# A causal bound at 64 tokens in a fused attention stage: 1280 instead of 1536 score columns a head step, new masks, sums and value layout

## The chip, the cores and the metric

The kernel runs as one program on one core of a Trainium2 chip. A core has five engines that run their own instruction streams in order and wait for each other on semaphores: TensorE (PE, matrix products into PSUM), VectorE (DVE), ScalarE (ACT), GpSimd (POOL) and SyncE (SP, which issues the transfers). The metric is device time in microseconds (us) of one execution; lower is better.

## The reference, cut to what matters

The network normalises and convolves a sequence, applies a mixture of experts, then attention, then the mixture of experts again, each with a residual sum. The change lies in the attention:

```python
def _L0_attn_b_ref(x, W_attn, W_proj):      # x: 16 batches, 256 tokens, 128 channels
    N_HEAD, N_QUERY_SETS = 16, 4            # 4 query sets share one set of keys and values, hd = 8
    qkv = x @ W_attn.T
    parts = jnp.split(qkv, N_QUERY_SETS + 2, axis=-1)
    causal = jnp.tril(jnp.ones((Tz, Tz), dtype=bool))
    for g in range(N_QUERY_SETS):
        att = jnp.einsum('bhqd,bhkd->bhqk', q, k) * scale
        att = jnp.where(causal, att, -jnp.inf)
        att = jax.nn.softmax(att, axis=-1)
        y = jnp.einsum('bhqk,bhkd->bhqd', att, v)
        outs.append(y.transpose(0, 2, 1, 3).reshape(Bz, Tz, C))
    return jnp.concatenate(outs, axis=-1) @ W_proj.T
```

## The kernel before, in words

The program has three parts in time: normalisation, convolution and the first expert layer; the attention; the second expert layer. The code that orders the attention is written out by hand: every engine runs a loop over `n` from 0 to 255, and each engine's loop says what it does at `n`.

**Numbering.** A batch `b` has 16 steps (`at = n % 16`). Its 16 heads are worked in four quads `c` of four heads, a head to a lane, and a quad has four steps `t = n % 4`. Below, t0 to t3 are these steps. A lane lives on 32 partitions of `qstack` and `kstack`.

**Scores.** `tensor_scores` (L1263) fills three banks of PSUM, 1536 columns, at each step: three products of 32 rows by 128 keys, 512 queries wide, from three lanes. There are two such PSUM tiles, so the scores of `n` wait for the exponentials of `n - 2` (`exped`). Keys of the first 128 positions meet all queries, keys of the second 128 only the queries of the second half.

**Exponentials.** `scalar_exp` (L1272) writes one tile of `prob`, a ring of 7 slots.

**Masks.** `gpsimd_mask` (L1279) zeroes the entries above the diagonal with affine selects, once a step, right behind that step's exponentials.

**Sums.** `tensor_weigh` (L1316) multiplies the weights by the values in `vstack`: four lanes, each on 32 columns of the array, all four into bank 7. The four groups of a quad are taken one quad later, one at t1, two at t2, one at t3 (`SUMS_Q`). The first one of quad `q` waits for `turned` (bank 7 is free) and for the masks of the quad's steps t0 and t1. `vector_turn` (L1324, L1327, L1329) transposes and normalises, `vector_rows` (L1339) transposes for the projection.

**Beside.** `tensor_beside` puts the next batches' work between scores and sums: the transposition `tensor_at_x` (L1113) at step 0, the query and key products `tensor_qk` (L1154) at 4, 8 and 12, the projection `tensor_project` (L1374) at 7 and 11, the values `tensor_v` (L1218) at 15. TensorE's order at a step is: scores, beside, sums:

```python
        for n in range(LAST):
            if n > 2:
                tensor_scores(e, n)
            tensor_beside(e, *STARTS[n])
            if n >= 4:
                at = n - n % 4 - 4
                for i in ((), (0,), (1, 2), (3,))[n % 4]:
                    tensor_weigh(e, at + i)
```

`vector_v` (L1237) copies the values from bank 6 to `vstack`; `tensor_at_x` of the next step 0 writes bank 6 again and waits for that copy (`v_copied`). `vector_bounds` (L1349, L1352) tests the reciprocals of the softmax sums, two instructions a batch. In the expert layers L937 and L1006 are the two products, L951 and L953 their activations. L493 is an exponential in the set-up.

## Time and profile before

| | |
|---|---|
| Time, median of 3 runs | 800.66 us (800.66 to 803.36) |
| Time of the profiled execution | 800.58 us |
| Its span, first to last instruction | 798.9 us |
| Busy: PE, ACT, DVE, POOL | 757.4, 719.9, 648.9, 560.2 us |
| Score products L1263, first and last of the loop's steps 3 and 255 | 248.31 and 604.68 us |

Busy time is the time in which an engine has an instruction under way. The rows of the trace give a start and a duration in us; for matrix products the end is modelled, so the start of the next group tells more than the duration. The 1.7 us between the time and the span lie outside the instructions.

### The profile page before, as it was taken

To read this page: it belongs to the slowest core of one execution; us is meant where nothing else is said; L and a number is where in the kernel's file an instruction comes from. 1 tells how busy PE (TensorE), PEld (TensorE's weight loads), DVE (VectorE), ACT (ScalarE), POOL (GpSimd) and SP (SyncE) were. 2 spreads that over 40 slices of the span, in tenths; PEclk is the share of its full clock that TensorE was granted. 3 is DMA by queue.
4 is the path that set the end of the run, shared out by engine and by line. 5 is a ranking of instruction groups with operands and counts; after the bars stand their busy time and mean duration, and the time that the engine had idled before them with its cause. 6 is when DMAs were issued, how large, how long until landed. Compare 5 with 4: busy or idle time off the path is not lost.

```text
span 798.9 us, 20426 instructions
## 1 busy us (share of the span) xinstructions
PE 757.4 (95%) x7674; PEld 412.7 (52%) x7674; DVE 648.9 (81%) x1917; ACT 719.9 (90%) x932; POOL 560.2 (70%) x685
## 2 busy tenths in 40 slices
PE   5898999999999999999999999999999999999996
PEld 3345667777774333333333333333334777677774
DVE  7998999999876667777778787788566898989885
ACT  5918999999999999999999999999997999899984
POOL 2897676655437888888898888888896445444442
PEclk9999999999999999999999999999999999999999
DMA  9110000000133333442444334433500000000000
GB/s 279 61 70 29 1 2 2 2 2 1 23 94 99 98 90 89 90 99 78 96 108 106 90 88 92 90 78 96 106 2 2 1 15 16 15 14 16 15 15 18
DMA packets 37962, 45.70 MB, mean 57 GB/s; under 512 B 6137, under 2 KB 23810, under 8 KB 37858
## 3 DMA queue, kind: packets, MB, share of 16 engines
q1 hardware_dynamic: 37858, 44.33, 22.4%
q8 instruction: 63, 1.03, 0.6%
q14 instruction: 41, 0.34, 0.2%
HBM read 27.53 MB, written 16.78 MB: 55 GB/s over the span
## 4 chain that ended last, share of the span: by engine, by line
PE 56%; ACT 18%; DVE 12%; issue 10%; POOL 2%; DMA 0%; ACTq 0%; DVEq 0%; POOLq 0%
PE psum L1006 15%; PE psum L937 14%; ACT prob L1272 13%; PE psum L1316 12%; PE psum L1263 5%; PE psum L1374 4%; DVE mixed L1025 4%; PE psum L1154 2%; ACT hidden_first L951 2%; ACT hidden_parts_first L953 1%; PE psum L686 1%; DVE hidden_parts_first L960 1%; POOL yhat L666 1%; DVE prod L656 1%; DVE stats L362 1%
## 5 line engine op out<-in xcount | busy, mean ns | idle before, releaser
L1272 ACT ACTIVATE prob<-psum 128x1536 f32<-128x1536 f32 x256 | 347.6, 1503 | 14.5 <-PE psum L1263 14.5
L1279 POOL TENSOR_SCALAR_AFFINE_SELECT prob<-prob 128x512 f32<-128x512 f32 (+3 forms) x448 | 304.8, 709 | 42.2 <-ACT prob L1272 32.1
L1316 PE MATMUL psum<-prob,vstack 128*32 128x256 f32 (+1 forms) x2048 | 204.9, 495 | 1.6 <-DVE o_tok L1324 1.6
L937 PE MATMUL psum<-xt_parts,w_parts 128*128 128x512 f16 x768 | 186.6, 379 | 0.0
L1025 DVE SCALAR_TENSOR_TENSOR mixed<-psum,comb_y,mixed 128x128 f32<-128x128 f32 x512 | 143.1, 339 | 1.5 <-PE psum L1006 1.5
L967 POOL TENSOR_TENSOR hidden_parts_second<-hidden_second,hidden_parts_second 128x512 f16<-128x512 f32 x64 | 77.2, 1207 | 93.6 <-ACT hidden_parts_second L953 93.6
L967 POOL TENSOR_TENSOR hidden_parts_first<-hidden_first,hidden_parts_first 128x512 f16<-128x512 f32 x64 | 79.4, 1241 | 73.2 <-ACT hidden_parts_first L953 73.2
L1263 PE MATMUL psum<-qstack,kstack 32*128 32x512 f16 x768 | 99.8, 385 | 9.1 <-ACT prob L1272 7.7
L1263 PEld LDWEIGHTS psum<-qstack,kstack 32*128 32x128 f16 x768 | 24.9, 91 | 157.3 <-ACT prob L1272 138.7
L937 PEld LDWEIGHTS psum<-xt_parts,w_parts 128*128 128x128 f16 x768 | 71.0, 98 | 64.0 <-issue 1.4
L951 ACT ACTIVATE hidden_second<-psum,b 128x512 f32<-128x512 f32 x128 | 88.3, 690 | 15.6 <-PE psum L937 12.1
L1006 PEld LDWEIGHTS psum<-w_parts,hidden_parts_first 128*128 128x128 f16 x1536 | 90.4, 98 | 19.4 <-issue 6.1
L1006 PE MATMUL psum<-w_parts,hidden_parts_first 128*128 128x128 f16 x1536 | 96.2, 219 | 3.8 <-DVE mixed L1025 3.4
L1006 PEld LDWEIGHTS psum<-w_parts,hidden_parts_second 128*128 128x128 f16 x1536 | 90.9, 98 | 16.2 <-issue 2.1
L1006 PE MATMUL psum<-w_parts,hidden_parts_second 128*128 128x128 f16 x1536 | 96.0, 219 | 1.0 <-POOL hidden_parts_second L967 0.5
L951 ACT ACTIVATE hidden_first<-psum,b 128x512 f32<-128x512 f32 x128 | 90.4, 706 | 7.0 <-PE psum L937 6.2
L953 ACT ACTIVATE hidden_parts_first<-psum,b 128x512 f16<-128x512 f32 x128 | 90.6, 708 | 0.0
L953 ACT ACTIVATE hidden_parts_second<-psum,b 128x512 f16<-128x512 f32 x128 | 88.4, 691 | 0.0
L1324 DVE STREAM_TRANSPOSE o_tok<-psum 128x512 f32<-128x512 f32 x64 | 45.9, 716 | 44.5 <-PE psum L1316 43.6
L1316 PEld LDWEIGHTS psum<-prob,vstack 128*32 128x32 f32 x2048 | 46.8, 108 | 52.8 <-issue 29.4
L960 DVE TENSOR_TENSOR hidden_parts_second<-hidden_second,hidden_parts_second 128x512 f16<-128x512 f32 x64 | 56.2, 878 | 18.9 <-ACT hidden_parts_second L953 18.8
L960 DVE TENSOR_TENSOR hidden_parts_first<-hidden_first,hidden_parts_first 128x512 f16<-128x512 f32 x64 | 48.9, 765 | 14.9 <-ACT hidden_parts_first L953 14.9
(148 smaller groups left out, 840.9 us busy)
## 6 DMA issues: line engine op xcount, KB each, us to landing
qstack<-qk_parts SPq DMA_DIRECT2D x128, 128.0 KB, 3.6
qk_parts<-parts SPq DMA_DIRECT2D x64, 192.0 KB, 3.1
kstack<-qk_parts SPq DMA_DIRECT2D x128, 32.0 KB, 3.5
stream<-u_folded SPq DMA_DIRECT2D x4, 512.0 KB, 8.0
kept_x<-stream SPq DMA_DIRECT2D x4, 512.0 KB, 2.7
out<-mixed SPq DMA_DIRECT2D x7, 256.0 KB, 2.3
w_whole<-L_ffn_W SPq DMA_DIRECT2D x1, 1024.0 KB, 8.9
taps<-c_taps SPq DMA_DIRECT2D x1, 640.0 KB, 7.1
```

What stands on the lines that cost most here:

```text
L937: last = e.matmul(bank(u % 4), m.w1[:, w_part, ex, cols], xt_parts[:, s, x_part, :], start=(n == 0), stop=(n == len(PRODUCTS) - 1))
L951: last = e.activation(m.hidden[:, r, k, :], bank(u % 4), ACT.Relu, scale=scale, bias=bias)
L953: last = e.activation(m.hidden_parts[:, r, 0, k, :], bank(u % 4), ACT.Relu, scale=scale, bias=bias)
L960: e.tensor_tensor(m.hidden_parts[:, r, 1, 0, :], m.hidden[:, r, 0, :], m.hidden_parts[:, r, 0, 0, :], ALU.subtract).then_inc(low_first, 1)
L967: e.tensor_tensor(m.hidden_parts[:, r, 1, 1, :], m.hidden[:, r, 1, :], m.hidden_parts[:, r, 0, 1, :], ALU.subtract).then_inc(low_second, 1)
L1006: last = e.matmul(down_place(m, ch, ex, t), h_[:, t * P:(t + 1) * P], w_, start=(n == 0), stop=(n == len(terms) - 1))
L1025: last = e.scalar_tensor_tensor(out=m.y[:, t0 + t, :], in0=down_place(m, ch, ex, t), scalar=comb_y[:, s, t, ex:ex + 1], in1=m.y[:, t0 + t, ...
L1263: last = e.matmul(to[:, i * BANK:(i + 1) * BANK], kstack[at, s, c, keys * P:(keys + 1) * P], queries, start=True, stop=True)
L1272: e.activation(prob[:, n % PROBS, :], psum[:, TILE * (n % 2):TILE * (n % 2 + 1)], ACT.Exp, scale=SCALE)\
L1279: return e.affine_select(kept, kept, [[0, kept.shape[1]], [0, 2], [sign, P]], ALU.is_ge, 0.0, base=0, channel_multiplier=-sign)
L1316: last = e.matmul(to[SLOT * lane:SLOT * (lane + 1)], vstack[:, b % 2, keys, first:first + SLOT], weights_of(n - t, lane, keys, pair), star ...
L1324: e.transpose(o_tok[:, r, :], bank(7)).then_inc(turned, 1)
```

## The change

The score matrix of each half sequence is cut once more, at 64 tokens. There are three kinds of score blocks for a head. EARLY: the first 64 keys of a half with that half's 128 queries, 512 columns over the four query sets, the two halves of the sequence on partitions 0 to 63 and 64 to 127. LATE: the last 64 keys of a half with its last 64 queries, 256 columns. ACROSS: the 128 keys of the first half with the 128 queries of the second, 512 columns, which need no mask. A step is then 512 + 512 + 256 = 1280 columns. Sequence halves change places inside the attention (three transpositions instead of two in `tensor_at_x`).

- Scores: EARLY and LATE blocks are made by two products each, one for each half of the sequence, which write 64 partitions.
- Exponentials: 1280 columns instead of 1536; the `prob` ring has 8 slots.
- Masks: six affine selects a quad instead of seven. The masks of t2 and t3 (their LATE blocks) are made together; the two selects of a mask lie apart in GpSimd's order.
- Sums: EARLY at t1, ACROSS at t2, LATE (256 columns) at t3 of the next quad, three groups instead of four.
- Values: 15 products instead of 6, three copies instead of one into a `vstack` of three kinds.
- `o_rows`: three transposes instead of one. Bounds: two instructions of 512 columns every four batches instead of two of 128 every batch.

```diff
-BOTH = None
-STEPS_Q = (((0, 0, 0), (1, 0, 0), (2, 1, BOTH)),
-           ((2, 0, 0), (3, 0, 0), (0, 1, BOTH)),
-           ((1, 1, BOTH), (3, 1, BOTH), (0, 0, 1)),
-           ((1, 0, 1), (2, 0, 1), (3, 0, 1)))
-
-SUMS_Q = ((0, 0, 1), (1, 0, 2), (1, 1, 2), (0, 1, 3))
+
+
+
+
+
+EARLY, LATE, ACROSS = range(3)
+BLK = P // 2
+
+STEPS_Q = (((EARLY, 0, 0), (EARLY, 1, BANK), (LATE, 2, 2 * BANK)),
+           ((EARLY, 2, 0), (EARLY, 3, BANK), (LATE, 1, 2 * BANK)),
+           ((ACROSS, 0, 0), (ACROSS, 1, BANK), (LATE, 3, 2 * BANK)),
+           ((ACROSS, 2, 0), (ACROSS, 3, BANK), (LATE, 0, 2 * BANK)))
+COLS = 2 * BANK + SETS * BLK
+SUMS_Q = (EARLY, ACROSS, LATE)
 STEPS_B = 4 * QUADS
-PROBS = 7
+SUMS_B = len(SUMS_Q) * QUADS
+MASKS_Q = 3
+PROBS = 8
+BOUNDED = 4
...
-        for h in range(HALVES):
-            last = e.transpose(bank(at_bank(b))[:, h * P:(h + 1) * P], normed[:, HALVES * b + h, :], eye[:])
+
+
+        for at, h in ((0, 1), (P, 1), (P + BLK, 0)):
+            last = e.transpose(bank(at_bank(b))[:, at:at + P], normed[:, HALVES * b + h, :], eye[:])
...
             e.wait_ge(attn_done, HALVES * (BATCH - 2))
-        for h in range(HALVES):
+        places = [(slice(0, P), P, ACROSS)]
+        places += [(slice(BLK * half, BLK * (half + 1)), P * half + BLK * kind, kind) for kind in (EARLY, LATE)
+                   for half in range(HALVES)]
+        for rows, first_token, kind in places:
             for i, (w_part, x_part) in enumerate(PRODUCTS):
-                last = e.matmul(bank(6)[:, h * P:(h + 1) * P], at_x[:, s, x_part, h * P:(h + 1) * P],
+                last = e.matmul(bank(6)[rows, kind * P:(kind + 1) * P],
+                                at_x[:, s, x_part, first_token:first_token + rows.stop - rows.start],
                                 wqkv_parts[:, w_part, SETS + 1, :], start=(i == 0), stop=(i == len(PRODUCTS) - 1))
         last.then_inc(v_up, 1)
 
...
+    def v_moves(b):
+
+        source = bank(6)[:, 0:3 * D].rearrange("p (k n d) -> p k n d", n=HEADS, d=HD)
+        places = vstack[:, b % 2, :, :, :, 0:HD]
+        for half in range(HALVES):
+            rows = slice(BLK * half, BLK * (half + 1))
+            yield places[rows, 0:2, :, half], source[rows, 0:2]
+        yield places[:, ACROSS, :, 0], source[:, ACROSS]
 
...
-        for i, (lane, keys, pair) in enumerate(STEPS_Q[t]):
+        for kind, lane, col in STEPS_Q[t]:
             at = slice(SLOT * lane, SLOT * (lane + 1))
-            if keys == 0:
-                queries = qstack[at, s, c, 2 * pair:2 * pair + 2, :].rearrange("p g (h q) -> p h g q", q=P)
-            else:
-                queries = qstack[at, s, c, :, P:SEQ]
-            last = e.matmul(to[:, i * BANK:(i + 1) * BANK], kstack[at, s, c, keys * P:(keys + 1) * P], queries, start=True,
-                            stop=True)
+            queries = qstack[at, s, c].rearrange("p g (h l q) -> p h l g q", h=HALVES, q=BLK)
+            if kind == ACROSS:
+                last = e.matmul(to[:, col:col + BANK], kstack[at, s, c, P:2 * P], queries[:, 0], start=True, stop=True)
+                continue
+            for half in range(HALVES):
+                rows = slice(BLK * half, BLK * (half + 1))
+                key = P * half + BLK * kind
+                if kind == EARLY:
+                    moving, place = queries[:, half], to[rows, col:col + BANK]
+                else:
+                    moving, place = queries[:, half, 1], to[rows, col:col + SETS * BLK]
+                last = e.matmul(place, kstack[at, s, c, key:key + BLK], moving, start=True, stop=True)
         last.then_inc(scored, 1)
 
     def scalar_exp(e, n):
         if n >= PROBS:
-            q, t = divmod(n - PROBS, 4)
-            e.wait_ge(weighed, 4 * q + (3 if t < 2 else 4))
+            e.wait_ge(weighed, len(SUMS_Q) * ((n - PROBS) // 4 + 1))
         e.wait_ge(scored, n + 1)
-        e.activation(prob[:, n % PROBS, :], psum[:, TILE * (n % 2):TILE * (n % 2 + 1)], ACT.Exp, scale=SCALE)\
...
+        e.activation(prob[:, n % PROBS, 0:COLS], psum[:, TILE * (n % 2):TILE * (n % 2) + COLS], ACT.Exp, scale=SCALE)\
...
+    def gpsimd_masked(e, kept, half):
+
+
+        sign = 1 if half else -1
+        return e.affine_select(kept, kept, [[0, n] for n in kept.shape[1:-1]] + [[sign, BLK]], ALU.is_ge, 0.0,
+                               base=BLK * half, channel_multiplier=-sign)
+
+    def mask_place(m):
+        q, t = divmod(m, MASKS_Q)
+        slot = (4 * q + t) % PROBS
+        if t < 2:
+            return prob[:, slot].rearrange("p (n l g q) -> p n l g q", n=3, l=2, q=BLK)[:, :, 0]
+        return prob[:, slot:slot + 2, 2 * BANK:COLS].rearrange("p n (g q) -> p n g q", q=BLK)
+
+    def gpsimd_second_half_mask(e, m):
+        q, t = divmod(m, MASKS_Q)
+        e.wait_ge(exped, 4 * q + t + 1 + t // 2)
+        gpsimd_masked(e, mask_place(m), 0).then_inc(half_masked, 1)
+
+    def gpsimd_first_half_mask(e, m):
+        e.wait_ge(half_masked, m + 1)
+        gpsimd_masked(e, mask_place(m), 1).then_inc(masked, 1)
 
     def gpsimd_mask(e, n):
-        t = n % 4
-        blocks = prob[:, n % PROBS, :].rearrange("p (n g q) -> p n g q", g=2, q=P)
-        e.wait_ge(exped, n + 1)
-        if t < 2:
-            gpsimd_masked(e, blocks[:, 0:3:2], False)
-            gpsimd_masked(e, blocks[:, 4:6], True).then_inc(masked, 1)
-        elif t == 2:
-            gpsimd_masked(e, blocks[:, 0:4], True)
-            gpsimd_masked(e, blocks[:, 4:5], False).then_inc(masked, 1)
+        q, t = divmod(n, 4)
+        if t != 2:
+            m = MASKS_Q * q + min(t, 2)
+            gpsimd_second_half_mask(e, m)
+            if m:
+                gpsimd_first_half_mask(e, m - 1)
...
+    def tensor_weigh(e, q, kind, last_of_quad):
+
+        b, c = divmod(q, QUADS)
+        if kind == EARLY:
+            if c == 0:
+                e.wait_ge(v_copied, b + 1)
+            if q == 0:
+                e.wait_ge(accum, EXPERTS * FFN_CHUNKS)
+            else:
+                e.wait_ge(turned, q)
+            e.wait_ge(masked, MASKS_Q * q + 2)
+        elif kind == ACROSS:
+            e.wait_ge(exped, 4 * (q + 1))
         else:
-            gpsimd_masked(e, blocks[:, 0:5:2], False).then_inc(masked, 1)
-
-    def weights_of(n, lane, keys, pair):
-
-        t, i = next((t, i) for t, banks in enumerate(STEPS_Q) for i, held in enumerate(banks)
-                    if held[:2] == (lane, keys) and held[2] in (pair, BOTH))
-        ring = prob[:, (n + t) % PROBS, i * BANK:(i + 1) * BANK]
-        return ring if keys == 0 else ring[:, pair * SEQ:(pair + 1) * SEQ]
-
-    def tensor_weigh(e, n):
-
-        b, c, t = step_of(n)
-        keys, pair, needs = SUMS_Q[t]
-        if n % STEPS_B == 0:
-            e.wait_ge(v_copied, b + 1)
-        if n == 0:
-            e.wait_ge(accum, EXPERTS * FFN_CHUNKS)
-        elif t == 0:
-            e.wait_ge(turned, n // 4)
-        e.wait_ge(masked, n - t + needs + 1)
-        to = bank(7) if keys == 0 else bank(7)[:, SEQ:2 * SEQ]
+            e.wait_ge(masked, MASKS_Q * (q + 1))
+        to = bank(7)[:, SETS * BLK:BANK] if kind == LATE else bank(7)
         for lane in range(LANES):
-            first = SLOT * (c * LANES + lane) + 2 * HD * (1 - pair)
-            last = e.matmul(to[SLOT * lane:SLOT * (lane + 1)], vstack[:, b % 2, keys, first:first + SLOT],
-                            weights_of(n - t, lane, keys, pair), start=(t == 0), stop=(t == 3))
+            last = e.matmul(to[SLOT * lane:SLOT * (lane + 1)],
+                            vstack[:, b % 2, kind, c * LANES + lane].rearrange("p h r -> p (h r)"),
+                            weights_of(q, kind, lane), start=(kind == EARLY), stop=last_of_quad)
...
+        for late in range(2):
+            e.transpose(rows[:, :, 1 - late], blocks[:, :, late])
+        e.transpose(o_rows[:, 1].rearrange("p g t -> p (g t)"), o_norm[:, 1].rearrange("p n r -> p (n r)"))\
          .then_inc(rows_up, 1)
...
-            if n >= 4:
-                at = n - n % 4 - 4
-                for i in ((), (0,), (1, 2), (3,))[n % 4]:
-                    tensor_weigh(e, at + i)
+            if n >= 4 and n % 4:
+                kind = SUMS_Q[n % 4 - 1]
+                tensor_weigh(e, n // 4 - 1, kind, kind == SUMS_Q[-1])
...
-        if b >= 2 and at in (2, 6):
-            vector_bounds(e, b - 2, at // 4)
+        if b >= BOUNDED and b % BOUNDED == 1 and at in (2, 6):
+            vector_bounds(e, b // BOUNDED - 1, at // 4)
...
+        gpsimd_first_half_mask(e, MASKS_Q * QUADS * BATCH - 1)
```

On TensorE, from the scores of t1 to the scores of t3 in one quad of batch 1, before (L1263 scores, L1316 sums; the size is partitions written by columns):

```order
L1263 MATMUL psum<-qstack,kstack 128x512 [waits exped]
L1263 MATMUL psum<-qstack,kstack 128x512 x2
L1316 MATMUL psum<-prob,vstack 32x512 [waits masked,out_turned]
L1316 MATMUL psum<-prob,vstack 32x512 x3
L1263 MATMUL psum<-qstack,kstack 128x512 [waits exped]
L1263 MATMUL psum<-qstack,kstack 128x512 x2
L1316 MATMUL psum<-prob,vstack 32x256 [waits masked]
L1316 MATMUL psum<-prob,vstack 32x256 x3
L1316 MATMUL psum<-prob,vstack 32x256 [waits masked]
L1316 MATMUL psum<-prob,vstack 32x256 x3
L1263 MATMUL psum<-qstack,kstack 128x512 [waits exped]
L1263 MATMUL psum<-qstack,kstack 128x512 x2
```

The same place in the changed kernel (L1286 and L1295 scores, L1360 sums):

```order
L1295 MATMUL psum<-qstack,kstack 64x512 [waits exped]
L1295 MATMUL psum<-qstack,kstack 64x512 x3
L1295 MATMUL psum<-qstack,kstack 64x256 x2
L1360 MATMUL psum<-prob,vstack 32x512 [waits masked,out_turned,v_copied]
L1360 MATMUL psum<-prob,vstack 32x512 x3
L1286 MATMUL psum<-qstack,kstack 128x512 [waits exped]
L1286 MATMUL psum<-qstack,kstack 128x512
L1295 MATMUL psum<-qstack,kstack 64x256 x2
L1360 MATMUL psum<-prob,vstack 32x512 [waits exped]
L1360 MATMUL psum<-prob,vstack 32x512 x3
L1286 MATMUL psum<-qstack,kstack 128x512 [waits exped]
L1286 MATMUL psum<-qstack,kstack 128x512
```

The score products of t1 write 64 partitions each, at t2 and t3 two products of 128 partitions are followed by two of 64, and the sums at t2 wait for the exponentials alone. The first sums of a quad, at t1, wait for `masked`, as before.

On GpSimd, the masks of one quad, t0 to t3, before (two selects each for t0, t1 and t2, one for t3):

```order
L1279 AFFINE_SELECT prob<-prob 128x2x256 [waits exped]
L1279 AFFINE_SELECT prob<-prob 128x512
L1279 AFFINE_SELECT prob<-prob 128x2x256 [waits exped]
L1279 AFFINE_SELECT prob<-prob 128x512
L1279 AFFINE_SELECT prob<-prob 128x1024 [waits exped]
L1279 AFFINE_SELECT prob<-prob 128x256
L1279 AFFINE_SELECT prob<-prob 128x3x256 [waits exped]
```

In the changed kernel, from t0 of a quad to t0 of the next (a 3x256 select belongs to the mask of t0 or of t1, a 2x256 one to that of t2 and t3):

```order
L1311 AFFINE_SELECT prob<-prob 128x3x256 [waits exped]
L1311 AFFINE_SELECT prob<-prob 128x2x256 [waits second_half_masked]
L1311 AFFINE_SELECT prob<-prob 128x3x256 [waits exped]
L1311 AFFINE_SELECT prob<-prob 128x3x256 [waits second_half_masked]
L1311 AFFINE_SELECT prob<-prob 128x2x256 [waits exped]
L1311 AFFINE_SELECT prob<-prob 128x3x256 [waits second_half_masked]
L1311 AFFINE_SELECT prob<-prob 128x3x256 [waits exped]
```

The selects that wait for `exped` are the first ones of a mask, those that wait for `second_half_masked` complete the mask before it. The 2x256 select that waits for `exped` waits for the exponentials of t3, and the 3x256 select behind it is the one that completes the mask of t1. The sums at t1 of the next quad wait for that count.

## Rows read from the trace of the kernel before

**Rows 1.** The page: busy times, and the group of the exponentials.

```profile
PE 757.4 (95%) x7674; PEld 412.7 (52%) x7674; DVE 648.9 (81%) x1917; ACT 719.9 (90%) x932; POOL 560.2 (70%) x685
...
L1272 ACT ACTIVATE prob<-psum 128x1536 f32<-128x1536 f32 x256 | 347.6, 1503 | 14.5 <-PE psum L1263 14.5
```

**Rows 2.** Windows view, 16 exponentials of one batch.

```profile
core 0: us, PE busy (x) PEld busy (x) DVE busy (x) ACT busy (x) POOL busy (x), PEclk, DMA share, GB/s
402.73:425.38 22.65, 22.35 (x216) 8.19 (x215) 17.37 (x40) 21.72 (x18) 20.09 (x30) 1.00 0.44 95
```

**Rows 3.** Timeline of PE: start us, us, instruction, count.

```profile
410.99 0.39 PE L1263 MATMUL psum<-qstack,kstack 32*128 32x512 f16 x3
411.32 1.16 PE L1374 MATMUL psum<-wproj,o_rows 128*128 128x128 f32 x8
412.40 1.07 PE L1316 MATMUL psum<-prob,vstack 128*32 128x512 f32 x8
413.40 0.39 PE L1263 MATMUL psum<-qstack,kstack 32*128 32x512 f16 x3
413.73 0.83 PE L1154 MATMUL psum<-at_x,wqkv_parts 128*128 128x256 f16 x6
414.49 0.39 PE L1263 MATMUL psum<-qstack,kstack 32*128 32x512 f16 x3
...
416.13 1.07 PE L1316 MATMUL psum<-prob,vstack 128*32 128x256 f32 x16
417.13 0.39 PE L1263 MATMUL psum<-qstack,kstack 32*128 32x512 f16 x3
...
423.27 0.51 PE L1218 MATMUL psum<-wqkv_parts,at_x 128*128 128x128 f16 x6
423.71 1.07 PE L1316 MATMUL psum<-prob,vstack 128*32 128x512 f32 x8
...
425.03 0.44 PE L1113 MATMUL psum<-eye,normed 128*128 128x128 f32 x2
425.57 0.39 PE L1263 MATMUL psum<-qstack,kstack 32*128 32x512 f16 x3
```

**Rows 4.** Waits in the attention: total us, times, longest.

```profile
PEld psum L1263 <- ACT prob L1272: 127.5, 194, 1.4
```

**Rows 5.** Timeline of POOL, ACT and DVE: single instructions and pairs.

```profile
249.63 1.46 POOL L1279 TENSOR_SCALAR_AFFINE_SELECT prob<-prob 128x1024 f32<-128x1024 f32 x2 [0.60 <-ACT prob L1272]
...
401.17 0.42 DVE L1237 TENSOR_SCALAR vstack<-psum 128x256 f32<-128x256 f32 x1 [0.70 <-PE psum L1218]
...
413.90 1.45 ACT L1272 ACTIVATE prob<-psum 128x1536 f32<-128x1536 f32 x1 [0.28 <-PE psum L1263]
...
415.42 4.98 POOL L1279 TENSOR_SCALAR_AFFINE_SELECT prob<-prob 128x512 f32<-128x512 f32 x7 [0.37 <-ACT prob L1272]
```

**Rows 6.** Instruction groups by form: selects and small exponentials.

```profile
L1279 POOL TENSOR_SCALAR_AFFINE_SELECT prob<-prob 128x512 f32<-128x512 f32 x256 | 158.0, 642 | 36.9 <-ACT prob L1272 31.5
...
L1279 POOL TENSOR_SCALAR_AFFINE_SELECT prob<-prob 128x768 f32<-128x768 f32 x64 | 56.3, 880 | 0.0
...
L493 ACT ACTIVATE powers<-powers 128x1024 f32<-128x1024 f32 x3 | 3.2, 1058 | 0.6 <-DVE powers L512 0.5
...
L493 ACT ACTIVATE powers<-powers 128x512 f32<-128x512 f32 x2 | 1.3, 630 | 1.4 <-DVE powers L512 1.3
```

**Rows 7.** Timeline of PE in the first expert layer.

```profile
241.35 1.46 PE L937 MATMUL psum<-xt_parts,w_parts 128*128 128x512 f16 x6
242.64 0.55 PE L1006 MATMUL psum<-w_parts,hidden_parts_first 128*128 128x128 f16 x7
```

**Rows 8.** Timeline of PE: step 3, step 255, and what follows.

```profile
248.31 0.39 PE L1263 MATMUL psum<-qstack,kstack 32*128 32x512 f16 x3
...
604.68 0.39 PE L1263 MATMUL psum<-qstack,kstack 32*128 32x512 f16 x3
...
608.34 1.47 PE L937 MATMUL psum<-xt_parts,w_parts 128*128 128x512 f16 x6
```

More of the change, by code:

```diff
@@ new lines, in gpsimd_first_half_mask, with weights_of @@
+    def gpsimd_first_half_mask(e, m):
+        e.wait_ge(half_masked, m + 1)
+        gpsimd_masked(e, mask_place(m), 1).then_inc(masked, 1)
+    def gpsimd_mask(e, n):
+        q, t = divmod(n, 4)
[4 more added lines that the diff above has]
+                gpsimd_first_half_mask(e, m - 1)
+    def weights_of(q, kind, lane):
+        t, col = next((t, at) for t, held in enumerate(STEPS_Q) for of, head, at in held if (of, head) == (kind, lane))
+        return prob[:, (4 * q + t) % PROBS, col:col + (SETS * BLK if kind == LATE else BANK)]
@@ L1638, in gpsimd_clear @@
         e.wait_ge(zeroed, 1)
[L1639 to L1640 removed]
+        e.memset(vstack[:, :, ACROSS, :, 0, HD:HD + 1], 1.0)
+        for half in range(HALVES):
+            e.memset(vstack[BLK * half:BLK * (half + 1), :, 0:2, :, half, HD:HD + 1], 1.0).then_inc(zeroed, 1)
+            e.wait_ge(zeroed, 2 + half)
         e.memset(in_bounds[:], 1.0).then_inc(zeroed, 1)
```

89 lines of the change are left out of this document (42 added, 47 removed).

## Prediction

> **What bounds the kernel now.** The change is confined to the attention, so I read that stage. The page says only that PE and ACT are both busy nearly always [rows 1]. The windows view of one batch, 16 steps, narrows it: in 22.65 us PE is busy for 22.35 and ACT for 21.72, with POOL at 20.09 and DVE at 17.37 [rows 2]. So two engines are level, and a gain must shorten both. The waits say how they hand over: PE's weight loads for the scores wait 194 times for exponentials, 127.5 us in all [rows 4], which lies largely under matrix products still running. The timeline gives the step: scores start, 0.32 to 0.33 us later the next group, then 1.00 us for a group of sums of 512 columns, or for two groups of 256 [rows 3]. A step with sums is 1.32 us of PE. From the scores of step 3 to those of step 255 there are 63 quads in 356.4 us [rows 8], 5.66 us each. Quads with a projection are longer (410.99 to 417.13, 6.14 us [rows 3]). GpSimd matters less than its 20 us suggest: its masks are wanted a step or more after they are ready, since the sums at t1 need only the masks of t0 and t1. That distance is what I looked at next.
>
> **The exponentials get shorter.** One isolated 1536-column exponential takes 1.45 us [rows 5]; 1024 and 512 columns took 1.06 and 0.63 [rows 6]. The slope is 0.76 to 0.84 us per 1000 columns, so 256 columns fewer save 0.20 to 0.22, and I take 1.24 us. Over 256 steps that is 54 us of ACT. It shortens the kernel only as far as nothing else sets the step.
>
> **The masks come later, and this sets the quad.** The order on GpSimd shows a 2x256 select that waits for the exponentials of t3, and behind it the 3x256 select that completes t1's mask. PE's EARLY sums at t1 of the next quad wait for that count. PE has just passed a scores group that needed the same exponential, so it arrives there 0.3 us after it ended, and the masks need two selects. A 512-column select takes 0.64 us, a 768-column one 0.88 [rows 6]; two in a row overlap by about 0.04 (1.46 for a pair of 1024 and 256, against 1.10 + 0.41 by the same shapes' usual length; the pair is in [rows 5], and I take only the overlap from it). So 1.47 us. This closes a loop, from the scores of t3 to those of the next t3:
>
> - Scores of t3, start to exponential: 0.50 (413.40 [rows 3] to 413.90 [rows 5], ACT idle before it). The end of the product to the exponential is 0.11 of it.
> - The LATE part behind ACROSS. Three 512-column score products in three lanes take 0.32 to the next group, whereas six full-array products without a change of shape take 1.29 [rows 7], 0.215 each. So streaming is 0.215 and each change of array shape costs about 0.105. LATE adds a change and 256 columns: 0.105 + 0.108 = 0.21.
> - Exponential 1.24; hand-over to POOL 0.07 (413.90 + 1.45 = 415.35, select at 415.42 [rows 5]); two selects 1.47; hand-over to PE 0.06, taken like the other.
> - EARLY sums 1.00; scores of t2 0.32 + 0.21 = 0.53; ACROSS sums 1.00; and the scores of t3 start.
>
> Sum: 0.50 + 0.21 + 1.24 + 0.07 + 1.47 + 0.06 + 1.00 + 0.53 + 1.00 = **6.08 us a quad**, against 5.66 now. PE is idle for about a microsecond of it in a light quad, ACT for more. ACT is no brake here: exponentials of t2 and t3 are ready 1.53 us apart.
>
> Is PE ever later than the masks? The masks allow EARLY 3.55 us after the scores of t3 (the first six terms). PE meanwhile has scores 0.53, LATE sums, two scores groups of 0.32, and what lies beside. LATE sums are 256 columns: two such groups take 1.00 in 16 products [rows 3], so (1.00 - 0.105)/2 + 0.105 = 0.55. That is 1.72 plus the work beside: projection 1.09 and query and key products 0.76 [rows 3] give 3.57. So 48 of the 63 quads take 6.08 to 6.10, together 292.3 us.
>
> **The quad across two batches** has the values and the transposition. Six value products take 0.44 [rows 3], (0.44 - 0.105)/6 = 0.056 each; 15 with one change between them take 15 x 0.056 + 0.21 = 1.05. They end 1.58 after the scores of t3. VectorE then copies in three instructions: 256 columns took 0.42 [rows 5], two of these and one of 128 for some 0.25 make 1.1, so the bank is free at 1.58 + 0.11 + 1.1 + 0.07 = 2.86. PE is there at 0.53 + 1.05 + 0.55 + 0.32 = 2.45 and waits. Three transpositions cost 0.76 (two took 0.54 [rows 3]: 0.22 each and the change), scores 0.32: EARLY starts at 3.94, not 3.55. The quad is 3.94 + 2.53 = 6.47, 15 times: 97.0 us.
>
> **Both ends.** 292.3 + 97.0 = 389.3 us instead of 356.4: +32.9. Behind step 255 the first expert product now starts 3.66 us after the scores [rows 8]. It will start at 3.55 + 1.00 + 0.55 = 5.10: +1.4. In front, the values and two transpositions of the first batches and the first steps' second shape add about 1. Sum +35.3 us.
>
> **At no cost:** three transposes for `o_rows` instead of one, and bounds tests of 512 columns every fourth batch, because VectorE has 5 us free in a batch [rows 2], and the sums' transposition it owes PE ends before the masks do. If that cover were gone, some 0.3 us in a quad of each batch would show, 5 us. The selects have rows of 64 entries instead of 128, which no row here prices: between the same rate and a fifth slower, 0 to 0.3 us a quad, or 0 to 19 us; I take 0, since 512, 768 and 1024 columns in different row counts lie on one line. The fast end, a fifth faster, would give 19 back. The prob ring with 8 slots never holds PE up: the exponential that needs a slot waits for LATE sums that lie ahead of its own scores on PE.
>
> **A rule weighed against the rows.** The rows show that three products in different shape groups cost 0.105 us more than their streaming [rows 3, 7], also from values (128 columns of the array) to sums (32 of them), where only the column count changes. The Trainium skill, TensorEngine Tiling (Array Packing), Key Properties, says that a change of the tiling mode, not of the tile, drains the engine. By that rule each scores group of t2 and t3 pays once more, and the sum stands at +35; were a change of the column count free, it would be the second rival's. The trace agrees for the shapes it has and does not show 32x128 to 32x64.
>
> **Rivals.**
> 1. *The masks hold, but ACROSS and LATE overlap.* Then 0.21 falls out twice of the loop: 5.66, with a projection 5.68, across batches 6.05. 32 x 5.66 + 16 x 5.68 + 15 x 6.05 = 362.8, +6.4, and with the ends **+9, 809 us**. For it: LATE uses another lane. Against it: the 0.105 above. Chance 0.14.
> 2. *The two column halves of a lane don't run together.* EARLY scores then stream 0.43 instead of 0.215, LATE 0.22. The loop is 6.30; with a projection PE is later: 0.64 + 0.55 + 2 x 0.535 + 1.85 = 4.11, and 4.11 + 1.00 + 0.64 + 1.00 = 6.75; across batches 7.1. 32 x 6.30 + 16 x 6.75 + 15 x 7.1 = 416, +60, and with the ends **about 862 us**. Against it: the four lanes of the sums read different weights on all 128 rows and still finish 512 columns in 1.00 us. The skill's same section says that tiles work in parallel, which agrees. Chance 0.08.
> 3. *Selects slower on short rows*: up to +19, **about 850 us**. Chance 0.08.
> 4. *Faster: the masks come in time.* Place: the two selects between t3's exponentials and EARLY. If they took under 1.16 us, and rival 1's overlap held, PE alone would set the pace: 22.35 busy, minus 4 x 0.45 for LATE, plus 0.61 for values and 0.22 for the transposition, 21.4 a batch instead of 22.65: about -18 for 15.75 batches, **783 us**. The point from which it decides: with rival 1's loop of 5.66, today's quad, every 0.1 us off the two selects' 1.47 gives 6 us, down to PE's 5.35 a quad; without that overlap they would have to take 1.05 before anything is gained. So it needs two things for which no row speaks. Chance 0.08.
>
> **How the numbers follow.** The sum's case has the rest, 0.62, and 828 to 845 as its own range (0.1 us of error in the loop is 6 us). It is made against the profiled execution's 800.6 us, which is the median's 800.7 as well: 800.6 + 35.3 = 836 us. The range reaches down to rival 1 and up to rival 3: 806 to 850. About half a per cent, 4 us, can be told from no change. Faster by more: rival 4 and nothing else, 0.08. Within: the low side of rival 1, 0.07. Slower: 0.85.
>
> **What the profile after would show.** The loop: the EARLY sums' waits name POOL in nearly every quad, about 1 us in light ones, where the profile before has almost none; quads of about 6.08 us, and 6.5 across batches; exponentials of 1.24 us with ACT idle at t3 and t2; the scores groups at t2 and t3 0.53 us to the next group, at t0 and t1 0.32; value products 1.05; the transposition waiting for the copy of the values. I would be wrong if quads stay at 5.3 to 5.7 with ACT idle short, if EARLY doesn't wait for POOL, or if the t0 and t1 scores stretch.

## The result, and the profile after

The changed kernel takes 862.66 us, the median of 4 runs (858.8 to 863.87), against 802.01 us for the kernel before in the same comparison: a ratio of 1.0745, 95% interval 1.0707 to 1.0783. It is **slower by 7.5%**. The forecast was slower, 836 us in 806 to 850. The profiled execution took 858.8 us, 58.2 more than that of before.

The page of the changed kernel: its busy times, then the granted clock in 40 slices, then groups (line, engine, operation, count; busy us and mean ns; idle time before and what ended it).

```profile
PE 782.7 (91%) x7834; PEld 422.6 (49%) x7834; DVE 659.2 (77%) x1955; ACT 682.4 (80%) x934; POOL 566.6 (66%) x623
...
PEclk9999999999998999999999899999899999999999
...
L1302 ACT ACTIVATE prob<-psum 128x1280 f32<-128x1280 f32 x256 | 309.4, 1237 | 106.2 <-PE psum L1295 105.0
...
L1360 PE MATMUL psum<-prob,vstack 128*32 128x512 f32 (+1 forms) x1536 | 186.3, 558 | 37.7 <-POOL prob L1311 35.9
```

ScalarE is busy for 37.5 us less than before [rows 1], as its exponentials went from 1503 to 1237 ns, and it now stands idle for 106 us before them, where it stood for 14.5 [rows 1]. The sums have a wait for GpSimd that they did not have. The slices of the clock no longer read 9 throughout. The waits between 258 and 650 us say the same (what waited, for what: us in all, times, longest). In these rows PEld is TensorE's load of weights, and `psum`, `prob`, `o_tok` and the like are the tiles written:

```profile
ACT prob L1302 <- PE psum L1295: 100.7, 162, 3.7
...
PE psum L1360 <- POOL prob L1311: 28.8, 32, 1.9
```

One quad in the timeline, from the scores of t3 to those of the next t3 (start us, duration us, instruction, count, and idle time with its releaser):

```profile
409.30 1.07 PE L1360 MATMUL psum<-prob,vstack 128*32 128x512 f32 x8 [1.25 <-POOL prob L1311]
...
411.83 0.39 PE L1286 MATMUL psum<-qstack,kstack 32*128 32x512 f16 x2
...
412.38 1.16 PE L1427 MATMUL psum<-wproj,o_rows 128*128 128x128 f32 x8
412.55 1.24 ACT L1302 ACTIVATE prob<-psum 128x1280 f32<-128x1280 f32 x1 [0.30 <-PE psum L1295]
...
413.47 0.64 PE L1360 MATMUL psum<-prob,vstack 128*32 128x256 f32 x8
...
413.86 1.52 POOL L1311 TENSOR_SCALAR_AFFINE_SELECT prob<-prob 128x512 f32<-128x512 f32 x2 [1.51 <-ACT prob L1302]
...
414.04 0.41 PE L1295 MATMUL psum<-qstack,kstack 32*64 32x512 f16 x6
...
414.38 0.83 PE L1168 MATMUL psum<-at_x,wqkv_parts 128*128 128x256 f16 x6
...
415.13 0.41 PE L1295 MATMUL psum<-qstack,kstack 32*64 32x512 f16 x6
...
415.52 1.07 PE L1360 MATMUL psum<-prob,vstack 128*32 128x512 f32 x8
...
416.52 0.39 PE L1286 MATMUL psum<-qstack,kstack 32*128 32x512 f16 x2
...
416.84 0.29 PE L1295 MATMUL psum<-qstack,kstack 32*64 32x256 f16 x2
...
417.06 1.06 PE L1360 MATMUL psum<-prob,vstack 128*32 128x512 f32 x8
...
418.06 0.39 PE L1286 MATMUL psum<-qstack,kstack 32*128 32x512 f16 x2
```

This is the loop of the prediction, with its links in order. The scores of t3 start at 411.83, the exponential at 412.55 and ends at 413.79. GpSimd starts at 413.86 and is through two selects at 415.38. The EARLY sums start at 415.52, the scores of t2 at 416.52, the ACROSS sums at 417.06, and the scores of t3 again at 418.06: 6.23 us. In this quad a projection and a query product (412.38, 414.38) fill TensorE's time before 415.52. In the quad ahead of it they don't: the EARLY sums at 409.30 stood idle for 1.25 us, with POOL as the releaser. I measured the loop on all 63 quads, from the start of one t3 exponential to the next: 6.22 to 6.23 us in 42 of them, 6.39 to 6.41 in twelve, and longer in nine, 6.74 to 9.95.

In eight of the nine TensorE's clock had fallen: its mean over the quad is 0.70 to 0.82. In the ninth, the one of 6.74 us, it is full. Windows of 6 us (the eighth figure of a row, the window counted as the first, is the granted clock), and TensorE in the timeline there:

```profile
475.00:481.00 6.00, 5.43 (x64) 1.88 (x62) 4.96 (x18) 4.88 (x4) 4.88 (x7) 1.00 0.59 143
...
487.00:493.00 6.00, 6.00 (x36) 2.55 (x29) 1.57 (x3) 2.11 (x3) 2.86 (x4) 0.50 0.50 65
```

```profile
484.86 1.07 PE L1360 MATMUL psum<-prob,vstack 128*32 128x512 f32 x8 [1.58 <-POOL prob L1311]
...
486.40 1.93 PE L1360 MATMUL psum<-prob,vstack 128*32 128x512 f32 x8
...
489.15 2.08 PE L1427 MATMUL psum<-wproj,o_rows 128*128 128x128 f32 x8
```

After an idle gap of 1.58 us at 484.86 the granted clock stands at 0.50, 1.2 instead of 2.4 GHz. The sums at 486.40 then take 1.93 us and a projection 2.08. An equal gap a hundred microseconds earlier left the clock up. This is the quad of 6.74 us:

```profile
384.21 1.07 PE L1360 MATMUL psum<-prob,vstack 128*32 128x512 f32 x8 [1.58 <-POOL prob L1311]
```

Not all of the time in the nine quads is the clock's. Gaps of 1.56 to 1.58 us, where the same place of other batches has 1.25, stand at 384.21, 484.86 and 588.43. They are in batches 5, 9 and 13, the ones with a bounds test on VectorE. Ahead of the first of them:

```profile
379.99 0.68 DVE L1405 SCALAR_TENSOR_TENSOR in_bounds<-rden,in_bounds 128x512 f32<-128x512 f32 x1
...
380.02 1.42 POOL L1311 TENSOR_SCALAR_AFFINE_SELECT prob<-prob 128x768 f32<-128x768 f32 x1
381.41 1.00 POOL L385 TENSOR_TENSOR rstd<-vareps,minus_half 128x4 f32<-128x4 f32 x1
```

Beside the test the select takes 1.42 us instead of 0.91. GpSimd has another operation behind it, and so comes late to the two selects that the EARLY sums need.

### The profile page after: what moved, and what is told of

Read it like the earlier page. It is cut to its first block, busy times and chain, and to the rows that moved or that the text cites. A ratio compares the mean times of both kernels' runs of the same rounds, so it can differ in the third digit from the quotient of the medians.

```text
span 857.1 us, 20723 instructions
## 1 busy us (share of the span) xinstructions
PE 782.7 (91%) x7834; PEld 422.6 (49%) x7834; DVE 659.2 (77%) x1955; ACT 682.4 (80%) x934; POOL 566.6 (66%) x623
## 4 chain that ended last, share of the span: by engine, by line
PE 61%; POOL 12%; DVE 11%; ACT 11%; issue 4%; DMA 0%; ACTq 0%; DVEq 0%; POOLq 0%
PE psum L1360 16%; PE psum L1015 14%; PE psum L946 13%; POOL prob L1311 10%; ACT prob L1302 7%; PE psum L1286 5%; PE psum L1295 4%; DVE mixed L1034 4%; PE psum L1427 2%; PE psum L1168 2%; ACT hidden_first L960 1%; ACT hidden_parts_first L962 1%; PE psum L695 1%; POOL rstd L385 1%; DVE hidden_parts_first L969 1%
## 5 line engine op out<-in xcount | busy, mean ns | idle before, releaser
L1302 ACT ACTIVATE prob<-psum 128x1280 f32<-128x1280 f32 x256 | 309.4, 1237 | 106.2 <-PE psum L1295 105.0
L1311 POOL TENSOR_SCALAR_AFFINE_SELECT prob<-prob 128x768 f32<-128x768 f32 (+1 forms) x384 | 312.2, 845 | 89.5 <-ACT prob L1302 87.3
L1360 PE MATMUL psum<-prob,vstack 128*32 128x512 f32 (+1 forms) x1536 | 186.3, 558 | 37.7 <-POOL prob L1311 35.9
L1295 PE MATMUL psum<-qstack,kstack 32*64 32x512 f16 (+1 forms) x1024 | 90.2, 348 | 1.4 <-ACT prob L1302 1.3
L1360 PEld LDWEIGHTS psum<-prob,vstack 128*32 128x32 f32 x1536 | 32.8, 109 | 71.5 <-issue 44.8
L1286 PEld LDWEIGHTS psum<-qstack,kstack 32*128 32x128 f16 x256 | 12.1, 91 | 112.3 <-issue 64.4
L1295 PEld LDWEIGHTS psum<-qstack,kstack 32*64 32x64 f16 x1024 | 28.4, 102 | 71.2 <-issue 53.5
```

The costliest lines, as they stand in the source:

```text
L1286: last = e.matmul(to[:, col:col + BANK], kstack[at, s, c, P:2 * P], queries[:, 0], start=True, stop=True)
L1295: last = e.matmul(place, kstack[at, s, c, key:key + BLK], moving, start=True, stop=True)
L1302: e.activation(prob[:, n % PROBS, 0:COLS], psum[:, TILE * (n % 2):TILE * (n % 2) + COLS], ACT.Exp, scale=SCALE)\
L1311: return e.affine_select(kept, kept, [[0, n] for n in kept.shape[1:-1]] + [[sign, BLK]], ALU.is_ge, 0.0, base=BLK * half, channel_multipli ...
L1360: last = e.matmul(to[SLOT * lane:SLOT * (lane + 1)], vstack[:, b % 2, kind, c * LANES + lane].rearrange("p h r -> p (h r)"), weights_of(q, ...
```

## The experiments

There are ten kernels. Of each, the median and range are given, then the ratio to the kernel before on the same chip with its 95% interval, and in places the mean granted clock of the profiled execution. Changes are to the changed kernel, or to the third experiment where it says so.

**1. The mask of t1 is completed behind the exponentials of t2.**

```diff
         q, t = divmod(n, 4)
-        if t != 2:
-            m = MASKS_Q * q + min(t, 2)
+        m = MASKS_Q * q + min(t, 2)
+        if t == 2:
+            gpsimd_first_half_mask(e, m - 1)
+        else:
             gpsimd_second_half_mask(e, m)
-            if m:
+            if m and t != 3:
                 gpsimd_first_half_mask(e, m - 1)
```

> The changed kernel, but the mask of t1 is completed behind the exponentials of t2 instead of behind those of t3; nothing else moves. Theory (the two selects between t3's exponentials and the EARLY sums set the quad): EARLY no longer waits for GpSimd, the quad falls from 6.22 us to what TensorE has to do, 22.6 us a batch by the changed kernel's own group starts (scores 2 x 0.34 + 2 x 0.54 a quad, sums 2 x 1.00 + 0.57, beside 5.3 a batch), which is 5.66 a quad; the clock stays at its full level; time 800 to 808 us. Rival (the new TensorE shapes cost the time, the mask wait only fills a gap that would be there anyway): 845 to 860 us, with PE idle named otherwise.

810.78 us (809.29 to 816.11), ratio 1.0138 (1.0093 to 1.0182), clock 0.993. The attention from the exponentials of step 3 to those of 255 takes 363.2 us instead of 410.3. So this one place in GpSimd's order held 52 of the 61 us between the medians. The largest waits between 258 and 590 us no longer name GpSimd as the releaser of sums. It is named once, for 0.6 us, against 27 times and 22.8 us in the changed kernel over the same window:

```profile
PEld psum L1286 <- ACT prob L1302: 71.3, 85, 0.8
ACT prob L1302 <- PE psum L1295: 53.9, 126, 1.4
```

It is 3 us above the range that I gave, so TensorE's own sum of 22.6 us a batch isn't quite reached: the attention's 63 quads are 5.77 us each.

**2. One array shape for all scores.** ACROSS is made like EARLY, as two products of 64 keys.

```diff
-            if kind == ACROSS:
-                last = e.matmul(to[:, col:col + BANK], kstack[at, s, c, P:2 * P], queries[:, 0], start=True, stop=True)
-                continue
             for half in range(HALVES):
                 rows = slice(BLK * half, BLK * (half + 1))
-                key = P * half + BLK * kind
-                if kind == EARLY:
+                key = P * half + BLK * kind if kind != ACROSS else P + BLK * half
+                if kind == ACROSS:
+                    moving, place = queries[:, 0], to[rows, col:col + BANK]
+                elif kind == EARLY:
```

> The changed kernel, but ACROSS scores are also made as two products of 64 keys each, so that all products of a step have one array shape. Mask order as in the changed kernel. Theory (a change of shape costs 0.1 us and keeps LATE from overlapping, and both t2 and t3 scores lie in the loop): scores of t2 and t3 take 0.34 instead of 0.54 to the next group, the loop loses 0.40 us to 5.82, 25 us in all; 832 to 838 us, or some us more if TensorE idles longer and its clock falls more often. Rival (the halves cost as much as the change of shape saves): 855 to 863 us.

832.31 us (830.89 to 834.45), ratio 1.0384 (1.0361 to 1.0407): 30 us less than the changed kernel. Six products now start at once, and the next group follows 0.34 us later, at t2 and at t3 too (451.85 to 452.19, 453.19 to 453.52):

```profile
451.85 0.41 PE L1294 MATMUL psum<-qstack,kstack 32*64 32x512 f16 x6
452.19 1.06 PE L1359 MATMUL psum<-prob,vstack 128*32 128x512 f32 x8
453.19 0.41 PE L1294 MATMUL psum<-qstack,kstack 32*64 32x512 f16 x6
453.52 1.16 PE L1426 MATMUL psum<-wproj,o_rows 128*128 128x128 f32 x8
```

The same two steps took 0.54 us in the changed kernel (416.52 to 417.06 above). The loop is 5.84 us in its usual quads, against 5.82 expected.

**3. Both edits.**

> Both edits: t1's mask completed behind t2's exponentials, and one array shape for all scores. Theory: nothing waits for masks, and TensorE has 22.6 - 8 x 0.2 = 21.0 us a batch against ScalarE's 17.9; 22.63 before; so about 25 us under the first experiment and under the kernel before: 775 to 782 us. Rival (GpSimd, 19.3 us of selects a batch plus a power of 1.1 in many, or VectorE becomes the next bound): 785 to 800 us.

793.22 us (792.52 to 793.99), ratio 0.9899 (0.9879 to 0.9919): 1% **faster than the kernel before**, and 11 us above the upper end of my expectation. The time falls in the rival's range, and of the rival's two causes VectorE has a part and GpSimd hardly any. GpSimd is busy for 314.6 of 344 us between 250 and 594 us and is the releaser of the sums nine times, for 3.8 us in all. TensorE's groups in a batch, start to start, add up to 21.0 us as I had it. The other 0.8 us of 21.75 are two gaps that VectorE ends, one at the projection and one at the transposition of tokens:

```profile
406.99 0.41 PE L1294 MATMUL psum<-qstack,kstack 32*64 32x512 f16 x6
...
407.58 1.16 PE L1428 MATMUL psum<-wproj,o_rows 128*128 128x128 f32 x8 [0.18 <-DVE o_rows L1391]
...
420.09 0.41 PE L1294 MATMUL psum<-qstack,kstack 32*64 32x512 f16 x6
...
420.95 0.52 PE L1124 MATMUL psum<-eye,normed 128*128 128x128 f32 x3 [0.46 <-DVE vstack L1261]
```

Behind scores the next group can start 0.34 us later. The projection starts 0.59 later, 0.25 us lost to the transposes for it, and the transposition of tokens 0.86 later, 0.52 us lost to the copies of the values. The rest of what is missing lies outside: 3.8 us more around the attention than before, most of it at its end.

**4. Idle time filled with thrown-away products**, in the changed kernel. They go to bank 7, which the sums behind them overwrite.

```diff
+            if q and c == 0:
+                for _ in range(4):
+                    e.matmul(bank(7), wqkv_parts[:, 0, 0, :], wqkv_parts[:, 0, 0:4, :].rearrange("p g d -> p (g d)"),
+                             start=True, stop=True)
             e.wait_ge(masked, MASKS_Q * q + 2)
```

> The changed kernel with four products of 512 columns, full array, thrown away, put ahead of TensorE's longest wait, the EARLY sums at step 5 of a batch (1.3 us idle, 1.6 and more in some batches). They take 0.86 us and two changes of shape of that idle time. Theory (that idle time lets TensorE's clock fall to half, which costs 15 us in the profiled run): the clock stays at 0.99 and more, the lengthened quads go, 843 to 850 us. Rival (the clock falls by itself or elsewhere, as it differs from run to run): clock 0.97 and 858 us or more, since work is added.

849.89 us (848.75 to 851.21), ratio 1.0609 (1.0584 to 1.0633), clock 0.987. **Adding work to TensorE took 13 us off the median.** The time is at the upper edge of the expectation and the clock is under it. The windows under experiment 10 tell why: at 487 to 493 us the clock is 1.00 where it was 0.50, but from 256 to 268 us it is 0.50, behind the first EARLY sums, at which nothing was filled.

**5. One select between the exponentials and the EARLY sums instead of two.**

```diff
             m = MASKS_Q * q + min(t, 2)
+            if t == 3:
+                e.wait_ge(exped, n + 1)
+                gpsimd_first_half_mask(e, m - 1)
             gpsimd_second_half_mask(e, m)
-            if m:
+            if m and t != 3:
                 gpsimd_first_half_mask(e, m - 1)
```

> The changed kernel, but at t3 the select that completes t1's mask goes first, still behind t3's exponentials, and the 512-column select of the next mask behind it. One select of 0.91 us lies between the exponentials and the EARLY sums instead of two of 1.52. Theory (the loop through GpSimd sets the quad): the loop falls by 0.61 us to 5.61, with the slower select of each batch's first quad 5.79; where TensorE has 1.1 us of projection and 0.76 of query and key products beside, it is the later one, 6.18, across batches 6.0; together some 35 us under the profiled 858.8 us of the changed kernel, with part of the clock's 15 us gone too: 812 to 828 us, between the changed kernel and the first experiment. Rival (any wait for t3's exponentials is enough, the number of selects behind it doesn't matter): 850 us or more.

824.78 us (823.68 to 831.75), ratio 1.0294 (1.0276 to 1.0311). It lies between the changed kernel and the first experiment, as the loop has it and as the rival doesn't. By quads of a batch, the medians are 5.63, 6.18, 5.85 and 6.04 us; I had 5.79, 6.18, 5.61 and 6.0; in the third a projection and a short query product make TensorE the later one, which I had overlooked. So the number of selects behind the exponentials is what counts, not the wait for them.

**6. The transposes for the projection one step earlier**, in the kernel of experiment 3.

```diff
+        if b and at == 4:
+            vector_rows(e, b - 1)
         if b + 2 < BATCH and at in (4, 8, 12):
...
-        if b and at == 5:
-            vector_rows(e, b - 1)
```

> Both edits of the third experiment, and VectorE's transposes for the projection one step earlier, ahead of the copies of the query and key products. In the third experiment the projection waits 0.47 us for them in each batch. Theory (TensorE bounds the heavy quads): 14 times 0.47 us less, 6 us under the third experiment, 786 to 790 us. Rival (the copies come 1.4 us later and the query and key products of the next quad or the transfers wait instead): 792 to 800 us.

795.44 us (793.04 to 795.57), ratio 0.992 (0.9901 to 0.9938): no gain, 2 us more if anything. The rival had the time and the late copies right, but the wait stands at the projection. It now waits for the second copy of the query and key products, which lies behind the transposes on VectorE:

```profile
406.45 0.67 DVE L1391 STREAM_TRANSPOSE o_rows<-o_norm 128x512 f32<-128x512 f32 x1
...
407.73 0.69 DVE L1198 SCALAR_TENSOR_TENSOR parts<-psum,parts 128x512 f16<-128x512 f32 x1
...
408.57 1.13 PE L1428 MATMUL psum<-wproj,o_rows 128*128 128x128 f32 x8 [0.37 <-DVE parts L1198]
```

**7. The softmax bounds checked for each batch again**, in the kernel of experiment 3 (`BOUNDED = 1`, and the calls of the kernel before).

> Both edits of the third experiment, with the softmax bounds checked for each batch as in the kernel before: two instructions of 128 columns a batch instead of two of 512 every four batches. Theory (VectorE has 8 us free in a batch, the bounds lie beside): 792 to 795 us, no difference that can be told. Rival (VectorE's 1.3 us a batch delay transposes that TensorE waits for): 798 us or more.

792.24 us (792.0 to 793.4), ratio 0.9894 (0.9878 to 0.9911), against 0.9899: that part of the change is worth nothing that can be told, in a kernel where the sums no longer wait for the masks.

**8. Exponentials of 1536 columns again**, in the kernel of experiment 3, the last 256 unused (`0:COLS` becomes `0:TILE`).

> Both edits of the third experiment, but each exponential runs over all 1536 columns, the last 256 of them unused. This takes back the shortening alone. Theory (TensorE is the bound in half of the steps, ScalarE with 1.12 us from start to start in the others; at 1.33 those grow by 0.2, about eight of sixteen steps): 1.0 to 1.9 us a batch more, 808 to 823 us. Rival A (TensorE alone sets the pace): 793 to 797 us. Rival B (ScalarE alone): 0.21 x 256 = 54 us more, 847 us.

796.54 us (794.71 to 797.56), ratio 0.9936 (0.9919 to 0.9952). The theory is wrong and rival A holds: with everything else in place, 0.21 us less in each of 256 exponentials gives 3 us. ScalarE is then busy for 49.16 of 50 us (sixth figure; the page's group below), and yet hardly costs anything: at 1.33 us from start to start sixteen steps are 21.3 us, under TensorE's 21.75. I had added the steps one by one. That the two PSUM tiles let a short step lend to a long one is my reading, and no run tests it.

```profile
300.00:350.00 50.00, 48.63 (x553) 18.18 (x547) 41.62 (x91) 49.16 (x38) 45.87 (x59) 1.00 0.46 95
```

```profile
L1301 ACT ACTIVATE prob<-psum 128x1536 f32<-128x1536 f32 x256 | 347.0, 1499 | 9.4 <-PE psum L1294 9.4
```

**9. The transposition of tokens one step later**, in the kernel of experiment 3, to take out its 0.52 us (`at == 0` becomes `at == 1` in two places).

> Both edits of the third experiment, and the three transpositions of the next batch's tokens one step later, at step 1 instead of step 0, with VectorE's copies of them. In the third experiment TensorE stands 0.52 us before them in each batch, for VectorE's three copies of the values, which use the same bank. Theory (TensorE sets the pace alone, so an idle gap taken out is time won): 13 times 0.52, 7 us under the third experiment, 785 to 788 us. Rival (as with the transposes for the projection, VectorE's later copies only move the wait, to the query and key products at step 4): 791 to 795 us.

791.03 us (788.86 to 793.26), ratio 0.9869 (0.9848 to 0.9891), the best of all, but only 2 us under experiment 3, whose interval it overlaps. The theory's 785 to 788 us is missed. The time is the lower edge of the rival's range, but the wait that the rival names, at the query and key products, doesn't appear. The transposition starts 0.86 us behind the scores of t0 (397.01 to 397.87), as in experiment 3 (420.09 to 420.95): the copies of the values still set its time. The scores of t1 now lie ahead of it and fill a part of the wait, 0.27 us of which is left:

```profile
397.01 0.59 PE L1294 MATMUL psum<-qstack,kstack 32*64 32x512 f16 x12
397.87 0.52 PE L1124 MATMUL psum<-eye,normed 128*128 128x128 f32 x3 [0.27 <-DVE vstack L1261]
```

**10. The two longest waits filled as well**: experiment 4 with eight products more before the first EARLY sums and before those of the last quad.

> The kernel of the fourth experiment, with eight more thrown-away products of 512 columns at the two longest waits of TensorE, the first EARLY sums (2.6 us idle in the changed kernel) and those of the last quad (2.7 us idle); they take 1.7 us each. With four products elsewhere the clock still stood at half from 256 to 268 us, behind the first wait. Theory (an idle TensorE lets its clock fall, and this is what is left of the 15 us): the granted clock is 0.99 or more, the attention from the exponentials of step 3 to 255 takes 395 us instead of 403.5, time 839 to 843 us. Rival (the fall is not tied to the idle time): clock 0.98 to 0.99 and 848 to 852 us.

845.98 us (844.03 to 850.42), ratio 1.0561 (1.0514 to 1.0608), clock 0.993. The clock is what I expected, the time 3 us above, and the attention takes 399.6 us instead of the 395 expected. Windows of the changed kernel, of experiment 4 and of this one, in that order:

```profile
256.00:262.00 6.00, 6.00 (x39) 1.42 (x36) 0.67 (x1) 2.76 (x3) 2.12 (x4) 0.57 0.01 3
```

```profile
256.00:262.00 6.00, 6.00 (x37) 1.43 (x34) 0.96 (x2) 2.84 (x3) 2.12 (x4) 0.50 0.01 3
262.00:268.00 6.00, 6.00 (x31) 1.07 (x28) 2.83 (x6) 3.35 (x3) 4.08 (x5) 0.50 0.00 0
487.00:493.00 6.00, 6.00 (x62) 2.55 (x58) 4.12 (x8) 4.69 (x4) 4.52 (x6) 1.00 0.31 86
```

```profile
256.00:262.00 6.00, 4.82 (x50) 1.53 (x48) 3.60 (x7) 4.73 (x4) 4.63 (x6) 1.00 0.04 4
...
268.00:274.00 6.00, 6.00 (x43) 1.58 (x39) 0.65 (x2) 2.31 (x2) 2.29 (x3) 0.51 0.55 131
```

The fall from 256 to 262 us is gone; another stands at 268 to 274, behind waits of quads that were not filled. One place, in a quad without filling in either kernel, shows that the length of the gap alone doesn't decide. In experiment 4 the sums behind it run at the lower clock, in experiment 10 they don't:

```profile
604.07 1.93 PE L1364 MATMUL psum<-prob,vstack 128*32 128x512 f32 x8 [1.27 <-POOL prob L1311]
...
601.96 1.07 PE L1365 MATMUL psum<-prob,vstack 128*32 128x512 f32 x8 [1.27 <-POOL prob L1311]
```

So idle time brings the falls, but which gap brings one can't be told from these runs.

## Why the prediction was right in direction and short in size

**What bounds the kernel; the loop.** Right. TensorE and ScalarE were level, the shorter exponentials alone are worth little (3 us in experiment 8), and the loop through GpSimd's two selects set the quad. Experiment 1 takes the loop away and 52 us go; experiment 5 takes 0.61 us of it and 38 go. One sign was overstated: the EARLY sums name GpSimd 32 times and not in nearly every quad, since where a projection and a query product lie beside, TensorE comes only just before the masks, as the sum had it (3.57 against 3.55). The link that rested on a judgement was the change of shape between ACROSS and LATE: it was 0.54 us to the next group, 0.53 predicted, and experiment 2, with one shape, has 0.34. The sentence that calls the case of a free change "the second rival's" means the first, in which ACROSS and LATE overlap. The Trainium skill's rule (TensorEngine Tiling (Array Packing), Key Properties) that a change of mode drains the engine agrees.

**The term "6.08 us a quad".** It is 6.22. Two links were short: the two selects took 1.52 instead of 1.47, since their starts lie 0.61 apart and the second takes 0.91 and not 0.88; and the hand-over to TensorE was 0.14, not the 0.06 that I had copied from ScalarE to GpSimd. In ten of the first quads of a batch the second select takes 1.08 and the loop 6.40. At the full clock, 47 x 6.22 + 16 x 6.40 = 394.7 us, where 389.3 stood: 5.4 us. It is 9.1 us too little for the 48 quads inside the batches and 3.7 too much for the 15 across them.

**The term "6.47 across batches".** 6.22. The 15 value products take 0.73, not 1.05. The price of 0.056 us holds for one product of full width, but the twelve of half width start in pairs, and a pair takes about as long, which no row of before showed. The three transpositions and their change of shape take 0.44, not 0.76:

```profile
401.92 0.52 PE L1124 MATMUL psum<-eye,normed 128*128 128x128 f32 x3 [0.45 <-DVE vstack L1261]
402.36 0.41 PE L1295 MATMUL psum<-qstack,kstack 32*64 32x512 f16 x6
```

They do wait for the copies of the values, as predicted. But TensorE comes to the EARLY sums before the masks, and this quad is like the others.

**No term for the clock.** This is the step that failed. I wrote that TensorE would stand idle for about a microsecond and took every product at the rows of before, which were all taken at the full clock. The attention takes 410.3 us and not 394.7: 15.6 us, nearly all in nine quads, of which the one at 484 us is shown above. About 13 of them are the clock's. That is an estimate. The first quad takes 7.43 us in experiment 10 at the full clock, 1.1 more than the first quads of other batches there, and the three bounds tests cost 0.34 us each (6.74 against 6.40), so about 2 us belong to late selects of GpSimd. Experiment 10 fills gaps and 10.7 of the 15.6 us go, in the attention of the profiled runs (399.6 us), with the selects and their order untouched; 1.4 of the 10.7 are the first quads of a batch, 6.31 instead of 6.40. The Trainium skill (TensorE: Matmul & The Clock Gate, Part 1: The HAM clock gate) has the rule that an idle TensorE goes to its lower clock. I should have weighed it. The trace agrees in direction, with 0.50 behind the gap of 1.58 us at 484.86; how much idle time it takes no run here shows.

**"Both ends."** +1.4 was predicted for the end and it is +3.7, from the last exponential to the first activation of the second expert layer. The last EARLY sums wait 2.7 us for masks, and behind that wait the clock stands at 0.50 from 664 to 667 us. The start is +0.9, as I had it.

The parts for the profiled runs: 35.3 predicted, 5.4 for the loops, 15.6 for the clock and the late selects in the attention and 2.3 for the end make 58.6, against 58.2. Without the 13 us of the clock the profiled run would have taken some 846 us, inside the range. The median is 4 us above the profiled run, with clocks of 0.966 to 0.970 in the other runs against its 0.977: more time at the lower clock.

**The rivals.** The second gave 862 us and the median is 862.66, and this is chance. Its mechanism, that the two column halves of a lane don't run together, is refuted by the 0.34 us of six products in experiment 2 and at t0 and t1 of the changed kernel (414.04 to 414.38). The first, overlap of ACROSS and LATE, is refuted by the 0.54. The third, selects slower on short rows by up to 19 us, is refuted in size: 512 columns take 0.66 instead of 0.64 us and 768 take 0.91 instead of 0.88, which is 3 us over the attention. The fourth, faster, needed the masks in time and scores without the price of LATE. Experiment 3 has both by other means and gives 793, against 783 in that rival. The two waits for VectorE and the ends are the larger part of the gap.

**"At no cost"** held for the bounds once the masks were out of the way (experiment 7). In the changed kernel their tests sit beside selects and cost 0.34 us three times, and the clock fell behind two of these three gaps. It didn't wholly hold for the three transposes and three copies: 0.25 and 0.52 us a batch show as soon as the masks are out of the way.

## What to carry to other kernels

When work is cut from two level engines, write down the loop that a tighter order closes through a third one, link by link: here GpSimd was never the busiest, yet two of its selects behind the last exponential of a quad cost some 50 us, the lower clock included, and putting one of them a step earlier gave them back. A sum made from rows of a full clock holds only while TensorE stays busy; if the forecast makes it idle, the forecast needs a term for the clock. And products of different array shape behind one another in one group cost twice: the change, and the overlap that is lost.

## What was unexpected of the hardware

- In the changed kernel the clock fell behind gaps of 1.45 to 2.68 us, but not behind the 1.58 us at 384.21, and gaps of 1.25 us as at 409.30 left it up. In experiment 4 it fell at one of 1.27 us. Four useless products of 512 columns ahead of the first EARLY sums of a batch made the kernel 13 us faster.
- Semaphore hand-overs differ by the engines: 0.07 us from ScalarE to GpSimd (413.79 to 413.86), 0.14 from GpSimd to TensorE (415.38 to 415.52).
- Six products of 32 rows by 64 columns in three lanes span 0.41 us together (451.85) and the next group follows in 0.34 us, against 0.32 for three of 128 columns [rows 3]: the split into halves is almost free.
